# Attention inside a fused layer: the row maxima moved with half as many transfers, the first pass six steps ahead instead of four, GpSimd's re-layout placed behind its splits

## The reference, cut to what matters

```
x_proj = x @ Wqkv + bqkv                      # 16 heads of 16 channels
q = x_proj[:, :, :C].reshape(B, n_head, T, hd)
k = x_proj[:, :, C:2 * C].reshape(B, n_head, T, hd)
v = x_proj[:, :, 2 * C:].reshape(B, n_head, T, hd)
att = jnp.einsum('bhtd,bhsd->bhts', q, k) * (1.0 / jnp.sqrt(jnp.float32(hd)))
att = jnp.where(causal, att, -inf)
att = softmax(att, axis=-1)
y = att @ v
y = transpose(y, (0, 2, 1, 3)).reshape(B, T, C)
return y @ Wproj + bproj
```

## Time and profile before

| what | value |
|---|---|
| runs, median | 4005.31 us |
| runs, lowest and highest | 3998.31 and 4005.49 us |
| the profiled execution's own time | 4003.91 us |
| its span in the trace | 4001.6 us |
| PE busy | 3698.8 us (92%) |
| DVE busy | 2974.0 us (74%) |
| ACT busy | 2208.5 us (55%) |
| POOL busy | 1661.2 us (42%) |
| mean granted clock of TensorE | 0.949 |

### The profile page before, as it was taken

The page is one execution under the profiler, slowest core; times in us unless marked ns, Lnnn a source line. Parts: engine busy times, 40 slices in busy tenths (PEclk is TensorE's granted clock), DMA queues, the critical chain, the costliest instruction groups (busy, mean ns, idle before and its releaser), DMA issues. The chain is left out here.

```text
span 4001.6 us, 76542 instructions
## 1 busy us (share of the span) xinstructions
PE 3698.8 (92%) x25550; PEld 2376.0 (59%) x25550; DVE 2974.0 (74%) x9275; ACT 2208.5 (55%) x4151; POOL 1661.2 (42%) x2027
## 2 busy tenths in 40 slices
PE   6998999997799999999999999999999997999997
PEld 5887766664455555555555555555555554766664
DVE  8997576675687778877778778777888883576675
ACT  1011555654265656656666666566666664565654
POOL 2332132323354555544655555545556520132323
PEclk9999999998698989989989999899999997999999
DMA  2333121211976866866767758766787751122111
GB/s 73 102 99 105 34 69 58 64 43 61 155 100 95 120 102 106 124 97 104 124 95 117 124 95 117 112 107 106 112 128 107 101 86 49 43 64 64 53 48 48
DMA packets 701462, 361.22 MB, mean 90 GB/s; under 512 B 305072, under 2 KB 668080, under 8 KB 701104
## 3 DMA queue, kind: packets, MB, share of 16 engines
q1 hardware_dynamic: 701104, 356.65, 49.3%
HBM read 204.49 MB, written 150.99 MB: 89 GB/s over the span
## 5 line engine op out<-in xcount | busy, mean ns | idle before, releaser
L1843 ACT ACTIVATE att_probs<-att_s 128x512 f32<-128x512 f32 x2304 | 1291.1, 599 | 851.1 <-PE att_s L1932 467.3
L1722 DVE CUSTOM_DVE_ANT_0 att_s<-att_s,att_above 128x384 f32<-128x384 f32 (+3 forms) x2048 | 962.6, 512 | 324.5 <-PE att_s L1962 318.9
L1982 PE MATMUL att_s<-att_qs,att_ks 49*128 49x512 f32 (+3 forms) x3072 | 925.2, 394 | 109.5 <-DMA att_qs<-att_row_max_T 47.2
L1962 PE MATMUL att_s<-att_ks,att_qs 48*128 48x512 f32 (+3 forms) x3072 | 1017.6, 417 | 7.2 <-DVE att_maxima L1725 3.7
L1982 PEld LDWEIGHTS att_s<-att_qs,att_ks 49*128 49x128 f32 x3072 | 487.0, 195 | 623.9 <-ACT att_probs L1843 413.5
L1725 DVE TENSOR_REDUCE att_maxima<-att_s 128x1 f32<-128x512 f32 x1024 | 673.9, 680 | 132.6 <-PE att_s L1962 129.7
L2010 PE MATMUL att_o_ps<-att_probs,att_vs 128*32 128x512 f32 (+3 forms) x6144 | 654.4, 523 | 0.7 <-ACT att_probs L1843 0.7
L1962 PEld LDWEIGHTS att_s<-att_ks,att_qs 48*128 48x128 f32 x3072 | 502.6, 196 | 25.3 <-DVE att_maxima L1722 7.9
L1097 PE MATMUL ffn_h2p<-ffn_h,ffn_w 128*128 128x512 f32 x768 | 364.8, 597 | 2.8 <-ACT ffn_h L968 0.6
L1932 PE MATMUL att_s<-att_mask,att_places 64*128 64x128 bf16 (+1 forms) x2560 | 341.0, 219 | 0.0
L1722 DVE DVE_READ_ACCUMULATOR2_ANT att_maxima<- 128x1 f32 x2048 | 287.9, 141 | 0.0
(11 more groups left out here) (292 smaller groups left out, 6167.0 us busy)
## 6 DMA issues: line engine op xcount, KB each, us to landing
att_staged<-qk_scratch SPq DMA_DIRECT2D x768, 128.0 KB, 7.2
qk_scratch<-att_parts SPq DMA_DIRECT2D x128, 512.0 KB, 3.5
ffn_x<-x SPq DMA_DIRECT2D x64, 512.0 KB, 5.3
ssm_x<-in_L_attn_a_x_dram SPq DMA_DIRECT2D x32, 512.0 KB, 3.7
x<-ssm_y SPq DMA_DIRECT2D x32, 512.0 KB, 3.0
x<-ffn_y SPq DMA_DIRECT2D x32, 512.0 KB, 2.9
att_x<-x SPq DMA_DIRECT2D x32, 512.0 KB, 12.6
v_scratch<-att_v_tok SPq DMA_DIRECT2D x32, 512.0 KB, 3.5
```

The costliest lines, as they stand in the source:

```text
L1722: last = v.tensor_tensor_reduce(scores, scores, above[:, CH - w:CH], 1.0, -3.0e38, ALU.add, ALU.max, to)
L1843: a(probs[u % PROBS][2 * g + p][:, 0:n], bank[:, 0:n], ACT.Exp).then_inc(exp_done, 1)
L1962: last = mm(bank[:, col:col + w], rows_of(qs[buf], g, KROWS, p, BT * blk, BT * (blk + 1)), rows_of(ks[buf], g, KROWS, p, t0, t1), start=k ...
L1982: last = mm(bank[:, col:col + w], rows_of(ks[buf], g, SHIFT + 1, p, BT * j, BT * (j + 1)), rows_of(qs[buf], g, SHIFT + 1, p, t0, t1), star ...
```

## The change

Three edits, all in the attention phase.

1. `move_max` copies both row groups in one transfer: the destination is rows 48 and 112 (a step of 64 partitions), the source 8 partitions instead of 4. Four transfers for a half instead of eight, and the three places that count them go from 128 to 64.
2. `LEAD` is 6 instead of 4. Units 8 and 17 fall on steps 2 and 11. `move_max` stands at 4 and 13 in SyncE's list instead of 6 and 15.
3. In slots with `q` = 3 `lay_out` stands at 9.2, 9.4, 11.2 and 13.2 instead of 6.3, 7.6, 10.2 and 12.2; in all others it stays.

```diff
-    LEAD = 4
+    LEAD = 6
-    LAY_OUT_AT, PREPARE_AT, PIECES = (6.3, 7.6, 10.2, 12.2), 6, 2
+    LAY_OUT_AT, LAY_OUT_BEHIND_X_AT = (6.3, 7.6, 10.2, 12.2), (9.2, 9.4, 11.2, 13.2)
+    PREPARE_AT, PIECES = 6, 2
...
                 def move_max(quad, buf, p):
                     sp.wait_ge(row_max_turned, 2 * quad + p + 1)
-                    for g in range(2):
-                        to = qs[buf][GROUP * g + SHIFT:GROUP * g + SHIFT + 1, NBLK * P * p:NBLK * P * (p + 1)].bitcast(F32)
-                        for a in range(4):
-                            sp.dma_start(to.rearrange("o (n a r) -> o n a r", a=4, r=32)[:, :, a, :],
-                                         row_max_T[p][32 * a + NBLK * g:32 * a + NBLK * (g + 1), :]).then_inc(max_moved[p], 16)
+                    to = qs[buf][SHIFT:SHIFT + GROUP + 1:GROUP, NBLK * P * p:NBLK * P * (p + 1)].bitcast(F32)
+                    for a in range(4):
+                        sp.dma_start(to.rearrange("g (n a r) -> g n a r", a=4, r=32)[:, :, a, :],
+                                     row_max_T[p][32 * a:32 * a + 2 * NBLK, :]).then_inc(max_moved[p], 16)
...
-                        tasks += [(6, lambda: move_max(4 * b + q + 1, (q + 1) % 4, 0)),
-                                  (15, lambda: move_max(4 * b + q + 1, (q + 1) % 4, 1))]
+                        tasks += [(4, lambda: move_max(4 * b + q + 1, (q + 1) % 4, 0)),
+                                  (13, lambda: move_max(4 * b + q + 1, (q + 1) % 4, 1))]
...
-                                tasks += [(LAY_OUT_AT[PIECES * side + e],
+                                tasks += [((LAY_OUT_BEHIND_X_AT if q == 3 else LAY_OUT_AT)[PIECES * side + e],
...
-                            dve.wait_ge(max_moved[p], 128 * quad)
+                            dve.wait_ge(max_moved[p], 64 * quad)
...
-                        pe.wait_ge(max_moved[step % 2], 128 * (quad + 1))
+                        pe.wait_ge(max_moved[step % 2], 64 * (quad + 1))
```

## The result

The changed kernel takes 3847.0 us (median of 4 runs, 3843.21 to 3855.52), the kernel before 4005.4 us on the same chip. The ratio is 0.961, with a 95% interval of 0.959 to 0.963: faster by 158 us. The forecast was 3856 us in a range of 3834 to 3930. The profiled execution took 3855.52 us, the slowest of the four, with a span of 3853.2 us.

The account below looks back on a forecast made before the run. TensorE, 92% busy, was taken as the bound, losing time to holes and the slow clock behind them. Gains of 85 + 22.6 + 40 - 6 + 4 + 5 = 150 us off 4003.91 gave 3854, predicted as 3856 us, range 3834 to 3930.

Parts of the forecast that it names:

- Which engine and why: TensorE in the attention: holes waiting for the moved maxima cost 2 us, the slow clock behind them some 11.
- The rival that the falls stay in the sparse slots: Slow stretches come from sparse q = 1 slots, so only holes are gained: 3956 us, chance 0.08; half staying, near 3905, 0.07.
- The sharp border: Of 14 q = 1 slots, the seven with the longest second-step hole fell; seven with 1.2 us or less stayed at 1.00.
- q = 1, 85 us: Fourteen q = 1 slots: without late maxima all take 30.95 us, from a sum of 518.44; gain 85 us, mostly clock.
- Merged transfers, 2.9 us for four: SyncE's issue of a half's maxima: four merged transfers take 2.9 us instead of eight's 5.71; bounds 1.4 and 5.7.
- q = 2, 22.6 us: Start of q = 2 slots: 0.54 us of wait for the maxima goes; 22.6 us over 14 slots, 15 if ScalarE holds it.
- q = 3, 40 us: GpSimd's split ahead of the copies shrinks TensorE's third-projection hole from 2.05 to 0.5 us: 37.5 over thirteen slots, 2.6 one earlier.
- The lead, -6 us (0 to -19): VectorE's heavier step 2 costs 0.1 us a slot, between 0 and 0.3; other pairing of matmuls costed at nothing.
- The ends, 4 + 5 us: First slot's 9.81 us wait shortened by 4 us (0 to 7); last four slots' falls and late maxima, 5 (0 to 7).
- three smaller falls: In the last four slots, clock falls that with late maxima there were to give 5 us (0 to 7).

Follow-up runs that it names:

- made holes: Three kernels: the change with SyncE holding back half 1's maxima at the end of q = 0 slots by a wait; 3905.0, 3926.4 and 3953.3 us.
- Version a: The change, with half 1's maxima held on SyncE until TensorE is three second-pass tiles short of the q = 0 slot's end; 3905.0 us, ratio 0.972.
- merge and layout: The kernel before with merged transfers and q = 3 re-layout behind the splits, lead 4, list places 6 and 15; 3830.6 us, ratio 0.955.
- layout only: The kernel before with only GpSimd's re-layout moved behind its splits in q = 3 slots; 3955.3 us, ratio 0.987.

## Why the prediction was right, point by point

**Which engine and why: right.** The prediction named slow clock behind holes at the moved maxima as the largest loss. The made holes settle it: 0, 8, 13 and 14 falls for none, 2.3, 2.5 and 3.6 us. The rival that the falls stay in the sparse slots is out: not one q = 1 slot of the change fell. The Trainium skill's page "TensorE: Matmul & The Clock Gate", section "HAM oscillation — how this bites in real kernels", on which that rival leaned, lets gaps of this size pass; these runs do not agree with it, since some 2.3 us was followed by a fall in 8 of 14 cases.

**The sharp border: too neat.** "Exactly those whose clock fell" held for the q = 1 slots of one execution. The q = 2 and q = 3 slots of the same execution already spoke against it. Here is slot 38, with the longest hole at the start of any q = 2 slot and clock 1.00 all through:

```profile
2467.63 0.47 PE L1982 MATMUL att_s<-att_qs,att_ks 49*128 49x512 f32 x1 [2.48 <-DMA att_qs<-att_row_max_T]
...
2464.27:2501.74 37.47, 34.06 (x293) 20.50 (x290) 28.76 (x97) 23.70 (x45) 23.76 (x23) 1.00 0.87 114
```

Slot 18 had 1.75 us of hole and 10.2 us of slow clock behind it. In q = 3, seven holes of 2.05 to 2.41 us passed (the earlier trace rows has one), while three of 1.8 to 2.0 us were followed by a fall. And where only the layout was changed, a q = 1 hole of 2.1 us passed at full clock, while two of 1.4 and 1.5 us were followed by 23.9 us at 0.50. The made holes show a longer one to make a fall likelier; no length tells which one.

**q = 1, 85 us: 81.4.** The mechanism is as told: cover at the slot's end (the last issue 0.9 to 4.3 us ahead of it, where 1.5 had been asked for), the store of v ahead of half 1, no hole. The 3.6 us missing are 14 x 0.26 us: slots of 31.22 instead of 30.96. That goes with the lead, whose other pairing of the matmuls the prediction had costed at nothing.

**Merged transfers, 2.9 us for four: 2.49 here,** 2.13 to 2.16 where nothing held them. The lower bound of 1.4 was not reached, the price of 5.7 was far off.

**q = 2, 22.6 us: 4.5. This is the step that failed.** Its 0.54 us at the slot's start was to come 14 times. But a calm q = 2 slot only went from 36.0 to 35.7, and three slots took 39 to 42 us because of the "issue" holes, 14.9 us together, of which the prediction had no term. Version a, with lead 6 and none of these holes, had 498.9 us here, a gain of 20.0, and merge and layout 500.1, a gain of 18.8. So the term itself was nearly right, and the issue holes undid it.

**q = 3, 40 us: 35.0** (32.7 and 2.3 for slot 3). The hole shrank to 0.53 us as worked out, and with lead 4 the slots are 33.27 us, against 33.3 forecast. With lead 6 they are 33.6, as in q = 1.

**The lead, -6 us (0 to -19): 16 by the medians,** and 25 in the profiled executions, or some 14 over the repeating slots without the issue holes. It was put down to VectorE, for which TensorE waits no longer than with lead 4. The medians lay inside the bounds by luck: the reason was not the one given. Nor did the prediction ask what each of the two cures was worth alone. Its own numbers held the answer: merging saves 2.9 us of issue where the hole was 2.24 us.

**The ends, 4 + 5 us: 8.8 + 19.0.** In slot 0 the maxima land after a hole of 1.5 us instead of 9.8; I had set this low, since I held the queue to be the limit. In the last four slots the end of one hole and its fall was worth 14.9 us, more than the sum set for all of them. The prediction had "three smaller falls" there. Two are small, 3.4 us each, but the third is the one of 41.0 us.

The repeating slots gave 117.4 us where the prediction had 85 + 22.6 + 37.5 - 6 = 139.1, and the ends, slot 3 among them, 30.4 where it had 2.6 + 4 + 5 = 11.6. The two errors, -22 and +19, nearly cancel, and that is luck: the total is closer than its terms.

## What to carry to other kernels

On this chip price a hole in dense TensorE work by the slow clock that may follow it: in the kernels with made holes 2.3 to 2.5 us of hole cost 2 to 6 us, and in the kernel before 2.2 us cost nearly 14. So look at the slots' clocks before the engines' shares, and at every single slot, the last too. When two edits cure the same wait, run each alone: here the cheap one was enough, and merge and layout with the old lead, at 3830.6 us, is the version to keep.

## What the runs showed that was not expected

- The slow clock behind a hole does not grow with it. In the q = 1 slots of the kernel before and of layout only (lead 4), holes of 1.4 to 3.0 us were followed by anything from nothing to 27.3 us of slow clock, and the hole of 2.0 us in the last slot of before by 41.0. With lead 6, holes of 2.3 to 3.6 us brought nothing to 10.2 us, and holes of 8 to 12.6 us brought 7.8 to 9.9 us once work had resumed. Whether the lead has a part in this is not shown.
- The same matmuls at the same full clock take 1% more of TensorE's time with the longer lead (30.64 and 30.95 us a slot). No wait in the profile tells it; only busy time over equal counts does.
- TensorE can stand still for 1.9 to 3.6 us with no releaser. In seven kernels with the same TensorE list nearly all of these holes stand at the same four places, and they come and go there. When 64 matmuls are added ahead, one of three stays. The cause is open.
- A transfer of twice the rows to SyncE costs no more to issue: 0.53 us for 2x8x32 undisturbed, where one of 1x8x32 took 0.68 to 0.71.
- Four small transfers issued behind six stack loads opened a hole of over 8 us, where the last of before's eight, issued ahead of them, landed 1.1 us after its issue.
